# Loading expert row tiles through a transposing DMA instead of turning them on TensorE

## What is computed

```python
x = x + tanh(g0) * attention(layernorm(x), ctx)        # softmax(q k^T), applied to rows of x
flat = layernorm(x).reshape(-1, 512)                   # 2048 tokens
logits = flat @ router_w.T                             # (2048, 8)
top_w, top_idx = top_k(softmax(logits), 2)
xb = flat.astype(bfloat16)                             # expert weights in bf16 as well
he = sigmoid(xb @ w_gate[e].T) * (xb @ w_up[e].T)      # 512 -> 352, for each expert e
de = he @ w_down[e].T                                  # 352 -> 512
x = x + tanh(g1) * (flat + shared(flat) + sum over the two experts of top_w * de)
```

## Time and profile before

| | |
|---|---|
| median of 3 runs | 337.62 us (336.86 to 339.15) |
| span of the profiled execution, first to last instruction | 339.6 us |
| TensorE busy (matmuls) | 298.9 us, 88% of the span |
| VectorE, ScalarE, GpSimd busy | 62%, 40%, 46% of the span |
| expert loop, first tile load issued to last wide product done | about 216 to 306 us |
| granted TensorE clock, mean | 0.954 |

### The profile page before, as it was taken

The page is one execution under the profiler, slowest core; times in us unless marked ns, Lnnn a source line. Parts: engine busy times, 40 slices in busy tenths (PEclk is TensorE's granted clock), DMA queues, the critical chain, the costliest instruction groups (busy, mean ns, idle before and its releaser), DMA issues.

```text
span 339.6 us, 6123 instructions
## 1 busy us (share of the span) xinstructions
PE 298.9 (88%) x1587; PEld 211.6 (62%) x1599; DVE 211.9 (62%) x580; ACT 136.3 (40%) x239; POOL 156.9 (46%) x237
## 2 busy tenths in 40 slices
PE   2678968999999999999999999699999999998280
PEld 1245845878687786878787787566666666664020
DVE  0147676748874667848357388647767677675191
ACT  1467166740667803657601562033343433333000
POOL 3041978166740384900687117115555656566100
PEclk9959977999999999999999999989999999999587
DMA  4999399512143021000029998224333333429498
GB/s 110 340 294 259 108 198 182 206 49 79 62 130 120 0 80 47 0 2 2 31 94 164 209 207 195 83 74 124 102 120 101 116 97 121 124 79 322 121 312 342
DMA packets 31444, 45.91 MB, mean 135 GB/s; under 512 B 3456, under 2 KB 21120, under 8 KB 31424
## 3 DMA queue, kind: packets, MB, share of 16 engines
q1 hardware_dynamic: 20992, 27.67, 26.7%
q0 software_dynamic: 10432, 17.99, 22.5%
HBM read 39.58 MB, written 14.72 MB: 160 GB/s over the span
## 4 chain that ended last, share of the span: by engine, by line
PE 67%; DMA 9%; POOL 6%; DVE 6%; issue 6%; ACT 2%; SPq 1%; POOLq 0%; ACTq 0%; DVEq 0%
PE bank L675 13%; PE bank L472 11%; PE bank L473 11%; PE bank L474 11%; PE bank L692 7%; POOL xg L398 4%; PE bank L467 4%; DMA acc<-x 4%; PE bank L483 3%; PE bank L667 3%; PE bank L683 2%; DMA z<-ysb,desti 2%; DMA zb<-z 2%; DVE acc L1264 1%; DVE probT_lo L983 1%
## 5 line engine op out<-in xcount | busy, mean ns | idle before, releaser
L888 ACT ACTIVATE sigc<-bank 128x352 f32<-128x352 f32 x39 | 18.1, 463 | 68.1 <-PE bank L675 68.1
L472 PE MATMUL bank<-lnT_hi,sgu_lo 128*128 128x512 f32 (+2 forms) x96 | 39.7, 414 | 1.6 <-DVE lnT_lo L983 1.6
L451 POOL DMA_INDIRECT z<-ysb,desti x36 | 36.1, 1002 | 9.7 <-issue 9.4
L473 PE MATMUL bank<-lnT_lo,sgu_hi 128*128 128x512 f32 (+2 forms) x96 | 38.5, 401 | 0.0
L474 PE MATMUL bank<-lnT_hi,sgu_hi 128*128 128x512 f32 (+2 forms) x96 | 38.4, 400 | 0.0
L675 PE MATMUL bank<-wgu_lo,xTb 128*128 x156 | 36.7, 317 | 0.0
L675 PE MATMUL bank<-wgu_hi,xTb 128*128 x156 | 36.7, 317 | 0.0
L398 POOL DMA_INDIRECT xg<-lnb,slot x32 | 31.9, 996 | 9.9 <-issue 7.3
L1231 DVE TENSOR_TENSOR hrow<-sigc,bank 128x352 bf16<-128x352 f32 x39 | 20.3, 521 | 25.2 <-ACT sigc L888 21.8
L387 POOL TENSOR_TENSOR hT_lo<-sig,hT_hi 128x512 fp32r<-128x512 f32 (+1 forms) x9 | 11.6, 1290 | 47.6 <-ACT hT_hi L798 47.5
L1237 DVE TENSOR_SCALAR ysb<-bank,wt 128x512 bf16<-128x512 f32 x39 | 29.2, 748 | 5.1 <-DMA z<-ysb,desti 2.6
(11 more groups left out here) (174 smaller groups left out, 650.1 us busy)
## 6 DMA issues: line engine op xcount, KB each, us to landing
xt<-xg SPq DMA_DIRECT2D x39, 129.0 KB, 2.1
xT_raw<-xT SPq DMA_DIRECT2D x4, 1024.0 KB, 7.8
acc<-x SPq DMA_DIRECT2D x4, 1024.0 KB, 10.0
out<-acc SPq DMA_DIRECT2D x16, 256.0 KB, 3.4
wgu_lo<-wguT POOLq DMA_DIRECT2D x2, 1408.0 KB, 14.0
wgu_hi<-wguT POOLq DMA_DIRECT2D x2, 1408.0 KB, 13.5
cx<-ctxT SPq DMA_DIRECT2D x4, 512.0 KB, 5.3
wd_sb<-wdT POOLq DMA_DIRECT2D x2, 1024.0 KB, 18.3
```

Source lines behind the costliest of these rows:

```text
L451: nc.gpsimd.indirect_dma_start(out=z, out_offset=bass.IndirectOffsetOnAxis(ap=desti[:, r:r + 1], axis=0), in_=ysb[:, r, :], in_offset=None ...
L472: pe.matmul(dst, a_lo, b_hi, start=first, stop=False)
L473: pe.matmul(dst, a_hi, b_lo, start=False, stop=False)
L888: act.activation(sigc[:, v, :], bank[2 * v][:, 0:I], ACT.Sigmoid).then_inc(s["csig"], 1)
```

## The change

The rows of a tile enter SBUF already turned, by one DMA with a transpose per tile, from the bf16 view of xg (xg_rows) into xTb, which now has four slots instead of two. The two words behind each row come by a second load of 8 bytes per row into xm. TensorE's rows_in, its PSUM bank and VectorE's copy to xTb are gone; wide waits for the load itself. SyncE's wait for a free slot is now on both the taken-over words (xev, now counted twice a tile) and the wide product of the slot's last tile (cgu). The rows of xg grow to 264 words, so that each starts at a multiple of 32 bytes, and GpSimd zeroes the six new words of the row buffers once, at the start (rowpads). The diff, cut to what changes:

```diff
-    ROW = N // 2 + 2
+    ROW = N // 2 + 8
     DST, WT = N // 2, N // 2 + 1
+    META = 2
...
+    xg_rows = xg.bitcast(BF16)
...
-        bankXT = bank[4][:, :].bitcast(BF16)
...
-        (xt, xTb, hrow, hTb, sigc, ysb), c_end = place((
-            ("xt", [P, SLOTS, ROW], U32), ("xTb", [P, 2, NT, P], BF16), ("hrow", [P, 2, IT * P], BF16),
+        (xm, xTb, hrow, hTb, sigc, ysb), c_end = place((
+            ("xm", [P, SLOTS, META], U32), ("xTb", [P, SLOTS, NT, P], BF16), ("hrow", [P, 2, IT * P], BF16),
...
-        xtb = xt[:].rearrange("p s r -> p (s r)").bitcast(BF16).rearrange("p (s r) -> p s r", s=SLOTS)
...
-            "sent packed xT_in padrows padout tabs cxt xev cgu csig ch ct cev cy yev dchain pchain didx za_in zsum comb outd").split()}
-        s_xl = [sem(f"xt_in{i}") for i in range(SLOTS)]
+            "sent packed xT_in padrows padout tabs cxt xev cgu csig ch ct cev cy yev dchain pchain rowpads didx za_in zsum comb outd").split()}
+        s_xl = [sem(f"xTb_in{i}") for i in range(SLOTS)]
+        s_ml = [sem(f"xm_in{i}") for i in range(SLOTS)]
...
                 if free is not None:
-                    sp.wait_ge(s["xev"], free)
+                    sp.wait_ge(s["xev"], 2 * free)
+                    sp.wait_ge(s["cgu"], free)
                 row = sp.value_load(erow[0:1, bass.ds(u, 1)], min_val=0, max_val=E * REG)
-                sp.dma_start(xt[:, slot_, :], xg[bass.ds(row, P), :]).then_inc(s_xl[slot_], 16)
+                sp.dma_start_transpose(xTb[:, slot_], xg_rows[bass.ds(row, P), 0:N]).then_inc(s_xl[slot_], 16)
+                sp.dma_start(xm[:, slot_, :], xg[bass.ds(row, P), DST:DST + META]).then_inc(s_ml[slot_], 16)
...
+            for c in range(TOP):
+                nc.gpsimd.memset(lnb[c][:, :, WT + 1:ROW], 0).then_inc(s["rowpads"], 1)
...
+                if b == 0 and c == 0:
+                    pool.wait_ge(s["rowpads"], TOP)
                 pool.wait_ge(s["order"], TOP * (b + 1))
...
-            def rows_in(u, r, q):
+            def wide(u, r, q, e):
+                v = r % 2
                 pe.wait_ge(s_xl[r], 16 * (q + 1))
-                at_least(pe, s["xev"], u)
-                for k in range(NT):
-                    mm = pe.transpose(bankXT[:, k * P:(k + 1) * P], xtb[:, r, k * P:(k + 1) * P], identb[:])
-                mm.then_inc(s["cxt"], 1)
-
-            def wide(u, v, e):
-                pe.wait_ge(s["xev"], u + 1)
                 at_least(pe, s["ch"], u - 1)
                 for half_ in range(2):
                     for k in range(NT):
-                        mm = pe.matmul(bank[2 * v + half_][:, 0:I], xTb[:, v, k, :], wgu(k, bass.ds(e, 1), half_ * I, I),
+                        mm = pe.matmul(bank[2 * v + half_][:, 0:I], xTb[:, r, k, :], wgu(k, bass.ds(e, 1), half_ * I, I),
                                        start=(k == 0), stop=(k == NT - 1))
...
-                if not known or u + 1 < NE:
-                    rows_in(u + 1, (r + 1) % SLOTS, q + 1 if r == SLOTS - 1 else q)
                 if not known or u < NE:
-                    wide(u, r % 2, ids[r + SLOTS - 1])
+                    wide(u, r, q, ids[r + SLOTS - 1])
             pe.wait_ge(s["lnTlo"], TT)
-            rows_in(0, 0, 0)
...
-            def rows_out(u, r):
-                dve.wait_ge(s["cxt"], u + 1)
-                at_least(dve, s["cgu"], u - 1)
-                V.tensor_tensor(dest[:, bass.ds(u, 1)], xt[:, r, DST:DST + 1], again[:, bass.ds(u, 1)], ALU.max)
-                V.tensor_copy(wt[:, bass.ds(u, 1)], xt[:, r, WT:WT + 1])
-                V.tensor_copy(xTb[:, r % 2], bankXT[:, 0:N].rearrange("p (k l) -> p k l", k=NT)).then_inc(s["xev"], 1)
+            def rows_out(u, r, q):
+                dve.wait_ge(s_ml[r], 16 * (q + 1))
+                V.tensor_tensor(dest[:, bass.ds(u, 1)], xm[:, r, 0:1], again[:, bass.ds(u, 1)], ALU.max).then_inc(s["xev"], 1)
+                V.tensor_copy(wt[:, bass.ds(u, 1)], xm[:, r, 1:2]).then_inc(s["xev"], 1)
...
-                    rows_out(u + 1, (r + 1) % SLOTS)
-
-            rows_out(0, 0)
+                    rows_out(u + 1, (r + 1) % SLOTS, q + 1 if r == SLOTS - 1 else q)
+
+            rows_out(0, 0, 0)
```

## The result

The changed kernel takes 363.53 us (360.01 to 364.86, 4 runs), the kernel before 338.38 us (336.86 to 339.24, 4 runs): a ratio of 1.0726, 95% interval 1.0643 to 1.0808, so 7.3% slower. The span of its profiled execution is 362.7 us. Each median is of all runs of its group, while the ratios leave out the few runs in which the whole kernel was over 1.5% slower than its fastest, so the two can differ by some tenths of a microsecond.

The account below looks back on a forecast made before the run. TensorE was taken to bound the expert loop. Removing 10.15 us and adding 0.6 us gave -9.5 us: 330.1 from the 339.6 us span, less 2.0 us to the median, so 328 us, range 325 to 332.

Parts of the forecast that it names:

- the second rival: Expert loop: the transposing load becomes the bound, by DMA engines (353 us) or by SyncE's issuing (350 us); chance 0.20.
- What it adds on SyncE's queue: SyncE's turn: 1.35 us plus 0.34 for the second load, 1.69; transposing issue taken as nothing extra, at most 1.0 us.
- the 0.45 us of room: SyncE's queue: 2.14 us step less 1.69 us turn, by which a transposing load's issue may exceed a plain one's.
- The second load: SyncE's queue: the two-word load beside each tile's rows, taken to add 0.34 us of issue per tile.
- What is removed from TensorE: Expert loop: 9.35 us of transposes plus 0.80 us of first eviction and hand-over go, 10.15 us; step 2.37 to 2.14.
- The pause at the loop's head stays: Head of each loop round: the 0.26 us in which TensorE waits for nothing shown was to remain unchanged.
- The DMA engines: Per tile: transposing load 1.2 us (low end 0.56), two-word load 0.49, sends 0.32, about 94% of a 2.14 us step.
- my middle case: DMA engines: transposing load moves as 512 pieces of 256 bytes at 38 ns, 1.2 us a tile.
- The third rival: Expert loop: transposing load in 64-byte pieces, 4.9 us of the engines a tile, +130 us, about 467 us; chance 0.16.
- The front: Before the first wide product: 1.79 us of transposes, eviction and hand-over go, 0.6 us of later first landing comes.
- its window: Landing of a tile's load: may take three times the 2.1 us of a plain load before the product needs it.
- SyncE without waits says issue: Sign in the profile after: if the wide product waits for loads and SyncE never waits, issuing is the bound.

## Why the prediction was wrong

I forecast 328 us and a gain; it was 363.5 and a loss. The bound moved, to SyncE's queue, which was the second rival's other way (2.7 us a tile, 350 us).

**The step that failed** is in "What it adds on SyncE's queue": "I take the low end, because the order of the changed kernel shows one instruction per tile". The count of instructions says nothing of their length. The instruction takes 1.22 us, 0.88 more than a plain load's, near the upper bound of 1.0 that stood beside it, and past the 0.45 us of room that I had worked out. What the runs put in its place: about 1.2 us per transposing load on SyncE's queue, nearly the same for the three sizes tried (1.18, 1.22 and 1.26 us).

**The second load** was mis-sized too: 0.34 us taken for the plain issue alone, 0.62 with the register work around it. The turn, by terms: 1.35 as before, 0.88, 0.62, and 0.12 for the rest, among it the second wait: 2.97 us. With 1.69 I was 1.3 us short. 39 x (2.97 - 2.37) = 23 us. In the two profiled executions the loop, from the first load's issue to the start of the last product's last matmul, takes 330.3 - 214.8 = 115.5 us instead of 309.7 - 216.2 = 93.5, 22 us more; the medians are 25 us apart, with an interval from 22 to 27. (The loop of the kernel before ends at 310 us and not at 306, as the table ahead of the prediction has it: 305.8 is where the chain leaves TensorE, two products early. Rows 3 miss one tile's transposes by it, 0.23 us.)

**What is removed from TensorE:** the transposes' share of the chain was read rightly, their worth was not. "The pause at the loop's head stays" is the wrong sentence. It grew from 0.26 to 0.51 us, and the products behind it ran slower: a step without transposes takes 2.23 us, not 2.14. The whole is worth 5.8 us, not 10.15, so the forecast would have been 3 to 4 us too low even with the transposing load as cheap as a plain one.

**The DMA engines** were feared too much. The packets fit pieces of 256 bytes, as in my middle case, but at 19 ns, not 38: 0.66 us a tile, near my low end of 0.56. The two-word load took 0.09 us and not 0.49, since its packets took 10 ns and not the 62 that I had drawn from rows 12. Both together took 0.72 us in the changed kernel, instead of 1.7. The third rival's 64-byte pieces, 2048 of them a tile, did not come: there are 544 packets.

The Trainium skill ("VectorE: DVE Perf Modes", "The three transpose paths") puts a 128x128 bf16 block at 1309 ns by the DMA crossbar. As a cost of every block that does not agree with this case: four blocks go out in an issue of 1.22 us, and eight in 1.26. The figure is near what one instruction costs SyncE here; that this is what the Trainium skill's figure measured, no run shows.

**The front** came out as forecast in number, but by luck. The first wide product starts at 217.7 us, 2.9 us after the first transposing load at 214.8; before it was 4.0 us after the plain one. That is 1.1 us less; 1.79 less 0.6 was the forecast. The 0.6 stood for engine time, 1.2 us instead of 0.56, and the engines took only 0.1 more on average. SyncE's issue of the first transposing load took 1.30 us, a plain one 0.34, which alone is more than the 0.6. The row, from the instructions that read the product's buffer:

```profile
L676 PE MATMUL bank<-wgu_lo,xTb x156: 310/313/501, 217.7 to 330.0; 128*128 x156
```

**Right too:** TensorE as the bound before; the next in line (VectorE, ScalarE, GpSimd) did not become one; the landing of a tile, 3.4 us from the start of its issue at 252.67 us in the chain, stayed inside its window; what the profile after would show if issuing were the bound ("SyncE without waits says issue") is what it showed.

What stays open: why the transposing load's issue is that long, and why single issues went down to 632 and up to 2290 ns, around the same median, when ScalarE issued loads beside them. With alternating plain and transposing loads, all on SyncE's queue, the record has 815 to 1293 ns. So a share that depends on what else is under way is not excluded:

```profile
L266 SPq DMA_TRANSPOSE xTb<-xg x39: 632/1191/2290, 214.7 to 298.8; - x39
```

## What to carry to other kernels

A queue that only issues is an engine with a budget: sum what one turn of it takes (reads of registers, register work, each issue by its kind), and set that against the step before giving it more; two kinds of load are two prices, and an unseen kind should be bounded by its upper price in the forecast itself. Taking cheap work off the engine that bounds a loop also takes away the time in which that engine's instruction stream runs ahead, so here the share of the chain (10 us) was more than the gain (about 6). Where a load must be issued more slowly, move what stands beside it to another issuing queue first: that alone turned 7% slower into 0.7% faster.

## What the runs showed of the hardware that I had not expected

- A transposing load from DRAM cost SyncE's queue 1.18 us for 128 x 256, 1.22 us for 128 x 512 and 1.26 us for 256 x 512 bf16 (medians); a plain load of 128 x 516 bf16 0.34 us.
- The engines carried a transposed tile of 128 x 512 bf16 in 544 packets of 19 ns each on average, 0.66 us of all 16 of them, against 0.56 us for the plain load: the transposing itself was cheap for them. A two-word load took 144 packets of 10 ns.
- A plain two-word load took 0.42 us to issue behind a transposing load on SyncE's queue, 0.33 us there behind a plain one (the run with unturned rows, median), and 0.35 us on ScalarE's:

```profile
L895 ACTq DMA_DIRECT2D xm<-xg x39: 344/350/393, 214.7 to 299.8; - x39
```
